# Feed-forward products in three rounded terms, two stack slots and new orders in a decoder layer kernel

## The reference, cut to what matters

```
x = x + attention(ln(x))       # 16 heads, q and k of 16, v of 64, softmax over the queries
x = x + cross(ctx, ln(x))      # 16 heads, exp feature maps of q, k, v; 64 context rows
x = x + ffn(ln(x))

# ffn
xr = mu_r*x + (1-mu_r)*x_prev  # x_prev: the row before, zero at the start
xk = mu_k*x + (1-mu_k)*x_prev
r  = sigmoid(xr @ W_r.T)       # all W are 256 x 256
k  = square(relu(xk @ W_k.T))
out = r * (k @ W_v.T)
```

## Time and profile before

| | us |
|---|---|
| median of 3 runs | 455.94 (455.62 to 457.22) |
| the profiled execution | 455.84 |
| its span in the trace | 454.0 |
| TensorE busy | 431.9 |
| VectorE busy | 373.3 |
| ScalarE busy | 298.8 |
| GpSimd busy | 134.4 |

### The profile page before, as it was taken

The page is one execution under the profiler, slowest core; times in us unless marked ns, Lnnn a source line. Parts: engine busy times, 40 slices in busy tenths (PEclk is TensorE's granted clock), DMA queues, the critical chain, the costliest instruction groups (busy, mean ns, idle before and its releaser), DMA issues.

```text
span 454.0 us, 8208 instructions
## 1 busy us (share of the span) xinstructions
PE 431.9 (95%) x2738; PEld 272.1 (60%) x2738; DVE 373.3 (82%) x689; ACT 298.8 (66%) x732; POOL 134.4 (30%) x181
## 2 busy tenths in 40 slices
PE   7989998999999999999999999999999999997785
PEld 5734355546556575666656575666555674586574
DVE  5677668778999989679999989678999878668875
ACT  3787776786797767746796667746898557423531
POOL 2241114134432351215231351214342413130610
PEclk9999999999999999999999999999999999999999
DMA  7986200443411001453300301453200200000001
GB/s 254 330 294 209 68 0 1 162 152 119 126 48 48 1 2 71 135 177 128 96 23 1 118 1 68 139 170 135 93 24 2 71 2 0 23 1 24 2 1 46
DMA packets 22561, 38.23 MB, mean 84 GB/s; under 512 B 2808, under 2 KB 7160, under 8 KB 22392
## 3 DMA queue, kind: packets, MB, share of 16 engines
q1 hardware_dynamic: 22520, 37.71, 24.9%
HBM read 23.02 MB, written 14.68 MB: 83 GB/s over the span
## 4 chain that ended last, share of the span: by engine, by line
PE 79%; DVE 8%; issue 5%; ACT 4%; POOL 1%; DMA 1%; SPq 0%; POOLq 0%; ACTq 0%; DVEq 0%
PE av_bank L731 22%; PE m_bank L663 10%; PE s_pair L717 8%; PE m_bank L667 7%; ACT e_sb L970 3%; DVE nmax L1169 3%; PE m_bank L867 3%; PE m_bank L879 2%; PE m_bank L939 2%; PE m_bank L783 2%; PE m_bank L804 2%; PE m_bank L928 2%; PE m_bank L748 2%; PE m_bank L950 2%; PE m_bank L767 1%
## 5 line engine op out<-in xcount | busy, mean ns | idle before, releaser
L970 ACT ACTIVATE e_sb<-s_pair,nmax 128x512 f32<-128x512 f32 x256 | 173.2, 690 | 54.0 <-DVE nmax L1169 53.4
L1169 DVE TENSOR_REDUCE nmax<-s_pair 128x2 f32<-128x1024 f32 x128 | 152.5, 1212 | 9.9 <-PE s_pair L717 9.3
L731 PE MATMUL av_bank<-e_sb,v_sb 128*64 128x512 f32 x512 | 124.0, 605 | 1.6 <-POOL v_sb L1441 0.8
L1441 POOL TENSOR_TENSOR v_sb<-v_sb,rsum 128x256 f32<-128x256 f32 x64 | 39.2, 612 | 183.6 <-DVE rsum L1177 175.8
L731 PEld LDWEIGHTS av_bank<-e_sb,v_sb 128*64 128x64 f32 x512 | 31.1, 136 | 55.1 <-issue 48.0
L970 ACT ACTIVATION_READ_ACCUMULATOR e_sb<-s_pair,nmax 128x1 f32 x256 | 53.1, 207 | 0.0
L717 PE MATMUL s_pair<-q_st,k_st 64*128 64x512 f32 x256 | 49.7, 453 | 2.1 <-ACT e_sb L970 1.5
L717 PEld LDWEIGHTS s_pair<-q_st,k_st 64*128 64x128 f32 x256 | 20.9, 184 | 50.8 <-issue 29.1
L1468 POOL TENSOR_TENSOR sx<-sx,xrec 128x512 f32<-128x512 f32 x24 | 24.8, 1044 | 47.0 <-DVE xrec L1350 47.0
L663 PE MATMUL m_bank<-wo_hi,ot_hi 128*128 128x256 f32 x120 | 34.3, 291 | 0.0
L667 PE MATMUL m_bank<-wo_lo,ot_hi 128*128 128x256 f32 x120 | 32.8, 279 | 0.0
(11 more groups left out here) (183 smaller groups left out, 816.1 us busy)
## 6 DMA issues: line engine op xcount, KB each, us to landing
q_st<-q_parts SPq DMA_DIRECT2D x31, 256.0 KB, 3.3
k_st<-k_parts SPq DMA_DIRECT2D x31, 256.0 KB, 3.1
k_parts<-qkt_hi SPq DMA_DIRECT2D x7, 512.0 KB, 3.1
k_parts<-qkt_lo SPq DMA_DIRECT2D x7, 512.0 KB, 4.2
q_parts<-qkt_hi SPq DMA_DIRECT2D x8, 256.0 KB, 2.0
q_parts<-qkt_lo SPq DMA_DIRECT2D x8, 256.0 KB, 2.3
out<-x_sb SPq DMA_DIRECT2D x8, 256.0 KB, 2.2
x_sb<-in_x SPq DMA_DIRECT2D x3, 512.0 KB, 5.5
```

The lines of the kernel that those rows point to most:

```text
L731: mm = pe.matmul(av_bank[n % AV_BANKS][64 * par:64 * par + 64, :], v_sb[:, m, 2 * p + par, :], e_sb[:, (4 * q + 2 * i + par) % E_RING, :], ...
L970: act.activation(e_sb[:, g % E_RING, :], s_pair[k // 2][:, k % 2, :], ACT.Exp, bias=nmax[:, g % 8:g % 8 + 1], accum_out=esum[:, q % 4, k:k ...
L1169: dve.tensor_reduce(nmax[:, at:at + 2], s_pair[i][:, :, :], AX_X, ALU.max, negate=True)\
L1441: pool.tensor_tensor(v_sb[:, m:m + 2, 2 * p:2 * p + 2, :], v_sb[:, m:m + 2, 2 * p:2 * p + 2, :], rsum[:, q % 4, :].rearrange("p (m h) -> p ...
```

## The change

- The FFN weights are loaded raw into pt_sb (a new load "ffn" on SP, which waits for both low cuts of the value weights) and cut once into wffn_hi (ScalarE) and wffn_lo (GpSimd).
- Each half gets three new units: mk, mr and ka, the high copy on ScalarE and the low subtraction on GpSimd of xk, xr and the squared activation. fr, fk and fv become 8 matmuls of by_high, then a wait for the low part, then 4 matmuls with it, all fp32r. mix waits for the low copies of the half before in place of the products.
- kact no longer has a tile of its own: it stands in mix_k, and in e_sb for batch 3.
- STACK is 2: q_st and k_st have two slots.
- All tables are written anew. In FIRST, the feature loads (feat on SP) move from behind x1 to behind the parts of qk (0, 1); qk (0, 1) and qk (1, 0) on TensorE come before first (0) and first (1); the cut of wo on GpSimd moves ahead of the first scaling, and the cut v1 behind the second. The feat unit on VectorE and ScalarE moves from the fifth quad to before the second quad's maxima and exponentials. In the tail, fk, fr and fv of batch 2, half 1, move behind z of batch 3. The warm-up matmuls are spread otherwise; as many as before, and they read kf in place of wffn_sb, with the same shape.

```diff
-STACK = 4
+STACK = 2
...
-    ("mix", -1, (0,), dict(dve=216)),
+    ("mix", -1, (0,), dict(dve=209)),
...
-    ("fr", -1, (0,), dict(pe=255, act=255)),
-    ("fk", -1, (0,), dict(pe=236, act=239, pool=234)),
+    ("fr", -1, (0,), dict(pe=260, act=251)),
+    ("fk", -1, (0,), dict(pe=234, act=224, pool=220)),
...
+    ("mk", -1, (0,), dict(act=215, pool=210)),
+    ("mr", -1, (0,), dict(act=223, pool=237)),
+    ("ka", -1, (0,), dict(act=245, pool=247)),
+    ("mk", -1, (1,), dict(act=256, pool=250)),
+    ("mr", -1, (1,), dict(act=288, pool=276)),
+    ("ka", -1, (1,), dict(act=318, pool=313)),
...
-    ("t2", (0,), dict(pe=96, act=96, dve=95)),
-    ("z", (0,), dict(pe=561)),
+    ("t2", (0,), dict(pe=59, act=64, dve=63)),
+    ("z", (0,), dict(pe=113)),
...
-    ("fr", (1,), dict(pe=77, act=77)),
-    ("fk", (1,), dict(pe=25, act=25, pool=14)),
-    ("fv", (1,), dict(pe=214, dve=197, sp=212)),
+    ("fr", (1,), dict(pe=276, act=210)),
+    ("fk", (1,), dict(pe=153, act=178, pool=64)),
+    ("fv", (1,), dict(pe=344, dve=251, sp=208)),
...
-    ("feat", (), dict(sp=105, dve=78, act=79)),
+    ("feat", (), dict(sp=97, dve=23, act=20)),
-    ("load", ("feat",), dict(sp=-634)),
+    ("load", ("feat",), dict(sp=-419)),
+    ("load", ("ffn",), dict(sp=30)),
+    ("cut", ("ffn",), dict(act=277, pool=279)),
...
-ATTENTION = dict(scores=11, weigh=42, max=(11, 12), exp=(15, 15, 17, 17), rsum=27, scale=12, ot_hi=38, ot_lo=44)
+ATTENTION = dict(scores=14, weigh=45, max=(11, 12), exp=(15, 15, 16, 16), rsum=26, scale=11, ot_hi=38, ot_lo=44)
...
             def fk(b, half):
                 unit = ("fk", b, (half,))
                 wait_bank(pe, unit)
-                pe.wait_ge(mixk_ready, 2 * b + half + 1)
+                if b == 0:
+                    pe.wait_ge(cut_lo["ffn"], 1)
+                pe.wait_ge(mix_cut["mk"][0], 2 * b + half + 1)
+                for mc in range(DC):
+                    cols = slice(mc * P, (mc + 1) * P)
+                    for c in range(DC):
+                        by_high(bank(unit)[:, mc * HALF:(mc + 1) * HALF], wffn_hi[:, 1, c, cols], wffn_lo[:, 1, c, cols],
+                                act_hi[:, c, :], None, (mc, c) == (0, 0), True)
+                pe.wait_ge(mix_cut["mk"][1], 2 * b + half + 1)
                 for mc in range(DC):
                     for c in range(DC):
-                        mm = pe.matmul(bank(unit)[:, mc * HALF:(mc + 1) * HALF],
-                                       wffn_sb[:, 1, c, mc * P:(mc + 1) * P], mix_k[:, c, :],
-                                       start=(c == 0), stop=(c == DC - 1))
+                        mm = pe.matmul(bank(unit)[:, mc * HALF:(mc + 1) * HALF], wffn_hi[:, 1, c, mc * P:(mc + 1) * P],
+                                       act_lo[:, c, :], start=False, stop=((mc, c) == (1, DC - 1)))
                 mm.then_inc(filled[uses[unit][0]], 1)
...
+            def high(which):
+                def part(b, half):
+                    n = 2 * b + half
+                    ready, hi, raw = {"mk": (mixk_ready, act_hi[:, :, :], mix_k[:, :, :]),
+                                      "mr": (mixr_ready, mixr_hi[:, :, :], mix_r[:, :, :]),
+                                      "ka": (kact_ready, act_at(b, half)[0], kact_at(b, half))}[which]
+                    act.wait_ge(ready, n + 1)
+                    if which != "ka" and n:
+                        last = {"mk": "fk" if n == 2 * B - 1 else "fv", "mr": "fr"}[which]
+                        wait_filled(act, (last, (n - 1) // 2, ((n - 1) % 2,)))
+                    act.activation(hi, raw, ACT.Copy).then_inc(mix_cut[which][0], 1)
+                return part
...
+            def low(which):
+                def part(b, half):
+                    hi, lo, raw = {"mk": (act_hi[:, :, :], act_lo[:, :, :], mix_k[:, :, :]),
+                                   "mr": (mixr_hi[:, :, :], mixr_lo[:, :, :], mix_r[:, :, :]),
+                                   "ka": act_at(b, half) + (kact_at(b, half),)}[which]
+                    pool.wait_ge(mix_cut[which][0], 2 * b + half + 1)
+                    pool.tensor_tensor(lo, raw, hi.bitcast(F32), ALU.subtract).then_inc(mix_cut[which][1], 1)
+                return part
```

More of the change, by code:

```diff
@@ L252 @@
+    ("mr", (0,), dict(act=-39, pool=-41)),
+    ("ka", (0,), dict(act=-10, pool=-20)),
+    ("mk", (1,), dict(act=63, pool=48)),
+    ("mr", (1,), dict(act=25, pool=0)),
+    ("ka", (1,), dict(act=214, pool=180)),
 ]
 FIRST = [
-    ("warm", (0, 2), dict(pe=-2864)),
-    ("warm", (1, 2), dict(pe=-59)),
-    ("warm", (2, 2), dict(pe=-393)),
-    ("ln1", (0,), dict(dve=-2796, pool=-2776, do=-2729)),
-    ("ln1", (1,), dict(dve=-2730, pool=-2768, do=-2729)),
-    ("cut", ("first",), dict(act=-990, dve=-983)),
@@ L271 @@
[L271 to L280 removed]
+    ("warm", (0, 2), dict(pe=-462)),
+    ("warm", (1, 2), dict(pe=-19)),
+    ("warm", (2, 2), dict(pe=-3088)),
@@ new lines @@
+    ("ln1", (0,), dict(dve=-3214, pool=-3204, do=-3206)),
+    ("ln1", (1,), dict(dve=-3208, pool=-3175, do=-3201)),
+    ("cut", ("first",), dict(act=-623, dve=-623)),
+    ("cut", ("qk",), dict(act=-3083, dve=-3093)),
+    ("t1", (0,), dict(dve=-3167, pe=-395, act=-3169)),
+    ("t1", (1,), dict(pe=-133, act=-3078, dve=-3023)),
+    ("first", (0,), dict(pe=-4, act=-59, dve=-12)),
+    ("first", (1,), dict(pe=3, act=-5, dve=2)),
+    ("qk", (0, 0), dict(dve=-580, sp=-667, pe=-10, act=-578)),
+    ("qk", (0, 1), dict(pe=-8, act=-421, dve=-421, sp=-425)),
@@ new lines @@
+    ("cut", ("v0",), dict(act=-104, dve=-110)),
+    ("cut", ("v1",), dict(act=28, pool=37)),
+    ("ld", (1,), dict(sp=-176)),
+    ("load", ("o",), dict(sp=-2238)),
+    ("ld", (2,), dict(sp=-3)),
+    ("load", ("x1",), dict(sp=-888)),
+    ("load", ("fc",), dict(sp=-205)),
+    ("load", ("rest",), dict(sp=9)),
+    ("load", ("feat",), dict(sp=-419)),
+    ("v", (0, 0), dict(pe=28, act=21)),
+    ("v", (0, 1), dict(pe=22, dve=23)),
+    ("v", (0, 2), dict(pe=11, act=9)),
+    ("v", (0, 3), dict(pe=37, dve=38)),
@@ L296 @@
[L296 to L305 removed]
+    ("cut", ("o",), dict(act=-3, pool=-7)),
+    ("cut", ("fc",), dict(act=184, pool=204)),
+    ("feat", (), dict(sp=97, dve=23, act=20)),
@@ new lines @@
+    ("kf", (0,), dict(pe=116, act=141)),
+    ("kf", (1,), dict(pe=147, act=161)),
+    ("warm", (3, 1), dict(pe=1253)),
+    ("warm", (4, 1), dict(pe=1332)),
+    ("warm", (5, 1), dict(pe=1519)),
+    ("warm", (6, 1), dict(pe=1467)),
+    ("warm", (7, 1), dict(pe=1349)),
+    ("warm", (8, 1), dict(pe=1431)),
+    ("warm", (9, 1), dict(pe=1082)),
+    ("warm", (10, 1), dict(pe=1248)),
+    ("warm", (11, 1), dict(pe=1238)),
+    ("warm", (12, 1), dict(pe=1102)),
+    ("warm", (13, 1), dict(pe=1410)),
@@ L588, in load @@
                     sp.dma_start(wfc_raw[:], wfc).then_inc(wfc_in, 16)
+                elif what == "ffn":
+                    for v in ("v0", "v1"):
+                        sp.wait_ge(cut_lo[v], 1)
+                    sp.dma_start(wffn_raw, wffn.rearrange("p k c n -> p (k c n)")).then_inc(wffn_in, 16)
                 elif what == "feat":
@@ L610, in qk @@
                 if b:
-                    for i in range(STACK):
-                        sp.wait_ge(stack_in[o][i], 16 * stacked((b - 1) * NP + 4 * c + i))
+                    for i in range(4):
+                        pair = (b - 1) * NP + 4 * c + i
+                        sp.wait_ge(stack_in[o][pair % STACK], 16 * stacked(pair))
                 for part in range(2):
```

536 lines of the change are left out of this document (267 added, 269 removed).

## The result

The change makes the kernel slower by half a per cent: 458.04 us median against 455.66 (22 runs each), ratio 1.0055, 95% interval 1.0041 to 1.0069. Predicted were 451.5 us, with a range of 446.5 to 456.5. The profiled execution of the changed kernel took 461.44 us, span 459.6, which is 3.4 us above its median; before 455.84 and 454.0.

The account below looks back on a forecast made before the run. It saw a start bound by the wait from maxima to exponentials, a middle bound by TensorE's instruction stream and a tail chained over all engines; -4.8 + 1.2 - 0.75 = -4.35 gave 451.5 us, range 446.5 to 456.5.

Parts of the forecast that it names:

- Products on TensorE, -4.8: Middle: 15 fr, fk and fv units each save 0.32 us as 12 fp32r matmuls; -4.8 us (0 to -7.0).
- The added copies (hidden in the middle): Middle: high copies on ScalarE (14.4 us) and low copies on GpSimd (30 us) fit into free time; 0 us.
- I leave it out of the sum: Shared port of VectorE and GpSimd: 0.4 us per meeting, hidden in the middle; 0.4 to 0.8 us, inside the range only.
- R4: Rival: late low copies stall each of 15 units on TensorE; at 0.7 us each 462 us, at 1.0 466.5; chance 0.09.
- The last chain, +1.1: Tail, last half, from mix_k's end to the gate: added copies lengthen 5.6 us to 6.7; +1.1 us.
- (a): Tail: fk of batch 2, second half, goes behind z, so the last weighing starts sooner; -0.35 us.
- (d): Tail: gate and update of batch 2, second half, now stand among VectorE's busy softmax work; +1.4 us.
- (b): Tail: fr and fv no longer precede z of batch 3 (-1.8); cross-attention scores come 2.3 us earlier in all.
- The warm-ups: Tail, term three: six, not twelve, warm-up matmuls ahead of the scores VectorE waits for; -0.6 us.
- Two slots, 0: Stacked q and k loads wait for the scores of the pair before last, with enough time; 0 us.
- The start, +1.2: Start: moved feature loads delay the second quad's first exponential from 26.33 to 27.0 to 28.4; net +1.2 us (0 to +3.5).

Follow-up runs that it names:

- plain_start: Changed kernel with its start order mended (456.43 us), every FFN product as 8 plain fp32 matmuls on high parts, copies and waits kept: 461.42 us, ratio 1.0109.
- port_shift: Changed kernel with start order mended (456.43 us), mr half 1's copy pair in batches 0 and 1 moved earlier on ScalarE and GpSimd: 455.16 us, ratio 0.9988.
- oldffn_start: Changed kernel with start order mended (456.43 us), FFN products plain fp32 as before the change, without high or low copies of activations: 454.78 us, ratio 0.9965.
- oldffn_stack4: oldffn_start with four score stack slots in place of two: 454.79 us against 454.78.
- feat_back: Changed kernel with feature loads ahead of the first q parts and their work after the fourth quad, as before the change: 458.78 us, ratio 1.0045.
- slots2_old: Kernel before the change with STACK 2 in place of 4, and its wait loop adapted: 469.79 us, ratio 1.0314.

## Why the prediction was wrong

It said -4.4 us and the medians say +2.4. Its own sign came true: the forecast was to be wrong if TensorE's idle time before 390 us grew by more than 3 us, and it grew by 5.4, from 9.40 to 14.82. By its steps:

**Products on TensorE, -4.8.** Right in mechanism and, but for one unit at the border, in the count of 15; too large by a quarter. The two units above take 1.41 and 1.47 us, 0.118 and 0.123 a matmul and not the 0.114 of the earlier trace rows, and the middle is 3.61 us shorter with the three terms than without (plain_start). In the tail they give 1.46, of which the sum had only the part in the chain.

**"The added copies (hidden in the middle)" and "I leave it out of the sum".** This is the step that failed, and the largest. It set 0 for the copies in the middle; they cost 2.55 us, where all else in the middle, products and orders together, gave back 2.9. ScalarE and GpSimd did have the slack that I read from the earlier trace rows. What the slack doesn't show is when they run: beside a 1.28 us subtraction on GpSimd a VectorE operation of 0.17 us took as long, and at two places behind it stands something for which TensorE waits. About 2.0 of the 2.55 us arise around these two places, and moving the copies there by a quad gave 1.27 us of the time back (port_shift). The other 0.5 come at the end of the middle, where GpSimd's own scalings stand behind low copies; no run moved these. The port had shown in the earlier trace rows, and I priced it at one or two meetings of 0.4 us in the tail, hidden in the middle; a meeting costs up to 1.12. I had asked only for VectorE operations with two SBUF operands, and so for mix_k and the updates; nmean has one.

The Trainium skill (SBUF — State Buffer, "Who interferes with whom") lists tensor_scalar, in a mode that uses both ports, among the VectorE operations that can contend with GpSimd, and I applied half of its rule. The trace agrees in that nmean ended with GpSimd's subtraction; in which mode it ran no row shows.

R4, low copies late for TensorE's own products, didn't happen in the middle: no gap inside the units shown.

**The last chain, +1.1.** It lost 2.83. I had the copies' durations right, one by one. Missing were the 0.91 us by which mix_k itself was stretched, ahead of the piece that I priced. That piece grew by 1.9, and of the 0.8 above the forecast 0.44 is the stretched last copy; the rest, some 0.4, I put down to the handovers between the engines, which no run priced. In the tail as a whole the copies cost 4.3 us and the products give 1.5 back.

**The rest of the tail.** My terms (a) to (d), -1.85 together, come out in their sum: without copies the tail is 2.2 shorter than before (oldffn_start). z of batch 3 follows the start of the last weighing by 10.14 us for 12.27, the 2 us of (a) and (b). The warm-ups, the gate and update weren't told apart.

**Two slots, 0.** Right for the middle and the tail of the new orders (oldffn_stack4); what decides is what queues behind a waiting load on SyncE, which I had named only in passing and only for the next batch. The old orders pay 14 us for it. Wrong in the start, where the q parts of the same batch stand behind the third pair's load: in feat_back that load waits 4.5 us for scores and holds them as late as the feature loads do. Its price by itself wasn't measured in the new start; in the old one it is 2.2 us of the profile (slots2_old).

**The start, +1.2.** The step I worked out, the second quad's exponential, came where I said. I stopped there and didn't follow the q parts that stand behind the feature loads and the third pair's load, nor who waits for them to land: ScalarE, 3.00 us. By the medians the start's order costs 1.6 us, near the forecast's 1.2, which is luck: it had neither this wait nor the clock, and in the profiled execution, with the halved clock, the start is 5.8 longer.

Together by the medians: new orders and plain products without copies -1.0 (454.78 against 455.82), copies +6.6, three terms -5.0, the start's order +1.6: +2.2, where after less before is +2.4. The sum closes by its making, each step being the difference of two variants; what it shows is the sizes. Against the forecast's 451.5 the missing 6.5 us are in the main 2.6 for the copies in the middle, 1.8 for copies less products in the tail (+2.9 for +1.1), 1.2 for the products in the middle and 0.7 for the middle's new order, for which it had no term.

## What to carry to other kernels

In this kernel an engine with slack still cost time where its work locked out another engine or sat in a chain; before adding operations to a slack engine, list what its neighbour runs in the same moments and who waits for that. Splitting an operand into parts paid where matmuls are the stream that bounds, and not at the end of the program, where the copies are a chain. When a load is moved in a queue, follow every entry behind it to its last reader, also the engine that waits to reuse the buffer. And when taking away a suspect changes nothing, as the feature loads in feat_back, look at what the same instruction waits for now: a second cause can stand right behind the first. One profiled execution is not the median; price an expectation from the median.
